# Attention cores: head 0 from SBUF, outputs kept in SBUF, one transfer per maximum, a banded core of its own, and an fp4 quantiser summed by TensorE

## The chip, the cores and the metric

The kernel runs on one core of a Trainium2 chip as one launch. TensorE (PE) multiplies matrices, VectorE (DVE), ScalarE (ACT) and GpSimd (POOL) work element by element, and SyncE's queue (SP) issues most transfers. The metric is the device time in microseconds, the median of several executions. SBUF is the on-chip memory of 128 partitions, PSUM the memory that matmuls write, DRAM lies off the core.

## The reference, cut to what matters

Tokens `x` (2048 of width 128) pass through eight residual layers, each `x = x + f(layernorm(x))`. The change touches the three attention layers with 16 heads of width 8 and the fp4 feed-forward layer.

```python
# L0 attention: each query sees itself and the 127 keys before it (banded)
scores = einsum('bhnqd,bhnkd->bhnqk', qb, kb) / sqrt(8); scores = where(allowed, scores, NEG)
out = einsum('bhnqk,bhnkd->bhnqd', softmax(scores), vb)        # allowed: 0 < distance <= 128
# L1 attention: the same over all keys, energy / sqrt(128).  L2 attention: causal, k <= q
# L0 feed-forward
def fp4_quant_dequant(x):            # blocks of 16 along the last dimension
    scale = maximum(max(abs(xb)) / 6.0, 1e-12)
    idx = searchsorted([0.25, 0.75, 1.25, 1.75, 2.5, 3.5, 5.0], abs(xb / scale))
    return [0.0, 0.5, 1.0, 1.5, 2.0, 3.0, 4.0, 6.0][idx] * sign(xb) * scale
h = silu(fp4_linear(x, w_gate)) * fp4_linear(x, w_up)           # hidden width 352
return fp4_linear(h, w_down)         # fp4_linear quantises both operands
```

## The kernel before

The program is a sequence of stages (`Stage`, one block of instructions for all engines each). A stage ends with a barrier of all engines, so nothing of one stage overlaps the next. The order of the work within a stage is written out by hand, engine by engine; semaphores join the engines, and each engine takes its own instructions strictly in order.

**An attention layer** is `layernorm_transpose`, `attention_front`, a core, `attention_normalise` and a projection. `attention_front` makes q, k and V for all heads. q and k are split into three bf16 parts each, so that nine bf16 products give an fp32 score, and the parts are stored to DRAM (`qparts`, `kparts`) by 12 transfers on SP (L1263). A core then treats head after head in two passes. Pass A computes all scores of the head with queries on the partitions, and DVE reduces each row to its maximum. The negated maxima are split in three bf16 parts, transposed by PE, copied to SBUF (`mT`) and laid by three transfers into rows 72 to 74 of `qh`, opposite three rows of ones in `kh`. Pass B computes the scores again, keys on the partitions, now with 75 rows, so that the maximum is already subtracted; ScalarE takes the exponential into `prob`. A third group of matmuls (L479, L791, L1117) multiplies `prob` with V and a column of ones into `psV`, four column chunks at partitions 0, 32, 64 and 96; ScalarE copies `psV` to `oh`, and SP stores output and denominators to DRAM in eight transfers a head. `attention_normalise` loads both back (L1380, L1381), inverts the denominators, spreads them with PE and multiplies.

The loads of `qh` and `kh` for a head broadcast the parts from DRAM on SP. Two or more heads are in flight: while PE does pass B of one head it takes units of pass A of the next in fixed slots (in the full-attention core 33 slots a head spread over 16 key blocks, the last one of which holds three), and the slot of the maxima transposition stands among them.

- The banded core (`attention_core`, stage l0a_core) treats a head as 31 blocks of 128 x 128: for each query block its own key block and the one before. In both passes each block gets a mask by a matmul of the identity with a 128 x 128 mask (L446, L467). Units are four blocks in A and eight in B. DVE reduces per query block (L578) and also splits the maxima (L590 to L596). POOL fills four `kh` with ones first (L410), 1.8 us each, and SP's first load waits for that.
- `wide_attention_core` (l1a_core) and `causal_attention_core` (l2a_core) have no masks in B; in the causal one POOL zeroes 16 diagonal blocks a head by `affine_select` (L1043). POOL splits the maxima in both (L1034 to L1037). DVE fills three `kh` with ones.

**fp4.** `Fp4` quantises a tile of 16-wide blocks: ScalarE takes magnitude and sign, DVE block maxima (L2067), scale (L2068), its inverse (L2069), the product with it (L2070), then counts thresholds in a chain of fused passes, `acc = (mag > mid) + acc` (L2072 to L2078), with one of the comparisons on POOL (L2053) while DVE does L2073, and ends with sign and scale (L2080, L2081). `l0_ffn` has stage l0w (weights 128 x 1120 and x, 128 x 2048) and stage l0h (hidden activations in four chunks of 128 x 1408: gate and up matmuls L2176, silu L2224, product L2247, quantisation, 12 transpositions L2185, ScalarE's copies L2214, 24 fp32 matmuls L2192, addition to X L2240).

## Time and profile before

Three executions took 3268.23, 3273.67 and 3277.10 us.

| what | us |
|---|---|
| median of three | 3273.67 |
| profiled execution, its own time | 3280.04 |
| its span in the trace | 3277.9 |
| ScalarE busy, POOL busy (whole span) | 1518.9, 549.0 |

Stages that the change touches, first to last instruction in the trace (us from the start of the span):

| stage | from | to |
|---|---|---|
| l0a_front (banded layer: projections, parts) | 31.55 | 61.68 |
| l0a_core | 62.49 | 317.02 |
| l0a_norm | 318.94 | 329.75 |
| l0w (fp4 weights and x) | 432.96 | 484.49 |
| l0h (fp4 hidden) | 485.26 | 611.19 |
| l1a_front (full attention) | 623.06 | 647.63 |
| l1a_core | 651.25 | 1420.22 |
| l1a_norm | 1422.16 | 1432.98 |
| l2a_front (causal) | 1746.61 | 1802.44 |
| l2a_core | 1805.67 | 2329.69 |
| l2a_norm | 2331.65 | 2343.42 |

Busy times count instructions that work, not the issuing of transfers. Matmuls are pipelined: one that is listed with 0.22 us starts 0.06 us after the one before it. A clock of 1.00 is TensorE's full 2.4 GHz, 0.5 is 1.2 GHz. What stands in brackets at the end of a row is how long the engine had been idle and what ended that.

### The profile page before, as it was taken

The page shows a single profiled execution, that of the slowest core. Times are in us where ns is not written, and L with a number is a line of the kernel's source. Part 1 is how long each engine was busy: PE and PEld are TensorE (multiplying, and loading weights), DVE is VectorE, ACT ScalarE, POOL GpSimd, SP SyncE. Part 2 cuts the span into 40 slices and gives each one's busy share as a digit, 9 for nine tenths or more (in the row PEclk, how much of TensorE's full clock was granted, in tenths as well). Part 3 has the DMA queues.
Part 4 walks back from the last instruction along what each step waited for, and adds up shares of the span by engine and source line. Part 5 has one row for each costly group of instructions (what it writes and reads, how often), then busy time and mean ns, then how long its engine had stood idle before and what let it go on. Part 6 is the DMA issues. An engine that isn't in the chain of part 4 may idle for free. (4 is left out here: it accounts for less than half of the span.)

```text
span 3277.9 us, 45624 instructions
## 1 busy us (share of the span) xinstructions
PE 2517.5 (77%) x16417; PEld 1220.7 (37%) x16417; DVE 1984.8 (61%) x3063; ACT 1518.9 (46%) x3040; POOL 549.0 (17%) x843
## 2 busy tenths in 40 slices
PE   2998523459999999957995799999677886766478
PEld 1776222312222222125674233333245545534423
DVE  2553477678888888531114677776285384458655
ACT  1232212217778777733432366666356356432211
POOL 3000011000000000000001111111174174104045
PEclk8998657659999999978997699999689998977689
DMA  2111000111111111002001000000110010000000
GB/s 69 47 50 40 1 9 0 44 56 39 38 37 39 43 43 43 3 17 52 1 1 38 29 23 26 26 26 11 46 34 5 1 30 2 1 6 2 1 20 13
DMA packets 57227, 82.88 MB, mean 25 GB/s; under 512 B 23114, under 2 KB 35564, under 8 KB 56620
## 3 DMA queue, kind: packets, MB, share of 16 engines
q1 hardware_dynamic: 57004, 79.97, 7.8%
q8 instruction: 132, 2.16, 0.3%
q14 instruction: 91, 0.75, 0.1%
HBM read 65.32 MB, written 14.02 MB: 24 GB/s over the span
## 5 line engine op out<-in xcount | busy, mean ns | idle before, releaser
L849 DVE TENSOR_REDUCE l1a_core_mpart<-l1a_core_psA 128x1 f32<-128x1024 f32 x512 | 601.5, 1220 | 96.8 <-PE l1a_core_psA L769 96.8
L831 ACT ACTIVATE l1a_core_prob<-l1a_core_psB 128x512 f32<-128x512 f32 x1024 | 552.1, 595 | 206.0 <-PE l1a_core_psB L780 204.4
L1159 ACT ACTIVATE l2a_core_prob<-l2a_core_psB 128x384 f32<-128x384 f32 (+3 forms) x656 | 316.0, 525 | 196.7 <-PE l2a_core_psB L1101 191.9
L1181 DVE TENSOR_REDUCE l2a_core_mpart<-l2a_core_psA 128x1 f32<-128x1024 f32 (+7 forms) x384 | 335.5, 909 | 118.0 <-PE l2a_core_psA L1088 68.0
L780 PE MATMUL l1a_core_psB<-l1a_core_qh,l1a_core_kh 75*128 75x512 bf16 x1024 | 312.0, 387 | 4.7 <-ACT l1a_core_prob L831 4.7
L791 PE MATMUL l1a_core_psV<-l1a_core_prob,l1a_core_vh 128*32 128x512 f32 x2048 | 274.4, 608 | 7.0 <-ACT l1a_core_oh L823 6.9
L769 PE MATMUL l1a_core_psA<-l1a_core_ka,l1a_core_qa 64*128 64x512 bf16 x1024 | 173.2, 403 | 67.9 <-DVE l1a_core_mpart L849 36.4
L1084 PE MATMUL l2a_core_psA<-l2a_core_kh,l2a_core_qh 72*128 72x512 bf16 (+3 forms) x640 | 181.3, 367 | 36.7 <-DMA l2a_core_kh<-kparts 31.3
L1101 PE MATMUL l2a_core_psB<-l2a_core_qh,l2a_core_kh 75*128 75x384 bf16 (+3 forms) x688 | 206.9, 349 | 2.8 <-DMA l2a_core_qh<-l2a_core_mT 2.6
L1117 PE MATMUL l2a_core_psV<-l2a_core_prob,l2a_core_vh 128*32 128x128 f32 (+3 forms) x1856 | 195.2, 444 | 15.0 <-ACT l2a_core_prob L1159 9.4
L1860 DVE SCALAR_TENSOR_TENSOR X<-l1e_psO,W,X 128x128 f32<-128x128 f32 x128 | 36.0, 344 | 220.6 <-PE l1e_psO L1817 220.6
L780 PEld LDWEIGHTS l1a_core_psB<-l1a_core_qh,l1a_core_kh 75*128 75x128 bf16 x1024 | 60.6, 97 | 292.6 <-ACT l1a_core_prob L831 271.6
L1849 ACT ACTIVATE l1e_h<-l1e_psH,l1e_b 128x512 f32<-128x512 f32 x128 | 87.9, 687 | 137.3 <-PE l1e_psH L1810 137.1
L1810 PE MATMUL l1e_psH<-XnT,l1e_w 128*128 128x512 f32 x256 | 118.6, 610 | 22.3 <-DMA l1e_b<-in_L_ffn_be 19.5
L1043 POOL TENSOR_SCALAR_AFFINE_SELECT l2a_core_prob<-l2a_core_prob 128x128 f32<-128x128 f32 x256 | 73.7, 292 | 359.3 <-ACT l2a_core_prob L1159 358.0
L578 DVE TENSOR_REDUCE l0a_core_mpart<-l0a_core_psA 128x1 f32<-128x128 f32 (+1 forms) x368 | 94.9, 329 | 57.0 <-PE l0a_core_psA L446 56.7
L557 ACT ACTIVATE l0a_core_prob<-l0a_core_psB 128x1024 f32<-128x1024 f32 x64 | 63.8, 998 | 138.1 <-PE l0a_core_psB L467 138.1
L769 PEld LDWEIGHTS l1a_core_psA<-l1a_core_ka,l1a_core_qa 64*128 64x128 bf16 x1024 | 45.9, 93 | 217.9 <-issue 112.6
L1817 PEld LDWEIGHTS l1e_psO<-l1e_w,l1e_h 128*128 128x128 f32 x1024 | 118.7, 192 | 13.4 <-issue 13.4
L1101 PEld LDWEIGHTS l2a_core_psB<-l2a_core_qh,l2a_core_kh 75*128 75x128 bf16 x688 | 62.2, 98 | 152.5 <-ACT l2a_core_prob L1159 90.3
L1817 PE MATMUL l1e_psO<-l1e_w,l1e_h 128*128 128x128 f32 x1024 | 118.8, 275 | 0.0
L2847 PE MATMUL l2f_qkv_psP<-l2f_w,XnT 128*128 128x512 f32 x192 | 96.2, 643 | 9.1 <-DVE V L2938 6.2
(632 smaller groups left out, 4444.4 us busy)
## 6 DMA issues: line engine op xcount, KB each, us to landing
l1a_core_qa<-qparts SPq DMA_DIRECT2D x64, 96.0 KB
l1a_core_ka<-kparts SPq DMA_DIRECT2D x32, 192.0 KB
l0a_core_kh<-kparts SPq DMA_DIRECT2D x48, 96.0 KB
l0a_core_qh<-qparts SPq DMA_DIRECT2D x48, 96.0 KB
l1a_core_qh<-qparts SPq DMA_DIRECT2D x48, 96.0 KB
l1a_core_kh<-kparts SPq DMA_DIRECT2D x16, 288.0 KB
l2a_core_qh<-qparts SPq DMA_DIRECT2D x48, 96.0 KB
l2a_core_kh<-kparts SPq DMA_DIRECT2D x16, 288.0 KB
```

The source lines that it names most:

```text
L769: ins = mm(ps[:, e * CH:(e + 1) * CH], qa[h % 2][rows, qb * P:(qb + 1) * P], ka[h % 2][rows, lo + e * CH:lo + (e + 1) * CH], start=True, s ...
L780: mm(psB[u % 3][:], kh[h % 3][0:QKM_ROWS, kb * P:(kb + 1) * P], qh[h % 3][0:QKM_ROWS, c * CH:(c + 1) * CH], start=True, stop=True).then_in ...
L791: ins = mm(psV[32 * c:32 * c + 32, :], vh[h % 2][:, kb, :], prob[(u + c) % (2 * PER_KB)][:], start=kb == 0, stop=kb == NT - 1, skip_group_ ...
L831: nc.scalar.activation(prob[u % (2 * PER_KB)][:], psB[u % 3][:], ACT.Exp, scale=scale).then_inc(b_exped, 1)
L849: nc.vector.tensor_reduce(mpart[:, n // 2, n % 2:n % 2 + 1], psA[i % 2][:], AX.X, ALU.max).then_inc(a_freed, 1)
L1084: ins = mm(ps[:, at * P:(at + nb) * P], qh[h % 3][0:QK_ROWS, place * P:(place + 1) * P], kh[h % 3][0:QK_ROWS, kb * P:(kb + nb) * P], start ...
L1101: ins = mm(out.rearrange("p (c n) -> p c n", c=groups), kh[h % 3][0:QKM_ROWS, kb * P:(kb + 1) * P], q4[:, c:c + groups, first * P:CH], sta ...
L1117: ins = mm(psV[32 * (c + i):32 * (c + i) + 32, first * P:CH], vh[h % 2][:, kb, :], prob[(NB * h + u) % RING][:, lo * P:(lo + 4 - first) * ...
L1159: nc.scalar.activation(prob[n % RING][:, 0:cols], psB[n % 3][:, 0:cols], ACT.Exp, scale=scale).then_inc(b_exped, 1)
L1181: ins = nc.vector.tensor_reduce(mpart[:, place, part:part + 1], psA[i % 2][:, lo * P:hi * P], AX.X, ALU.max)
L1810: nc.tensor.matmul(psH[j][:], w1[:, e, j * P:(j + 1) * P], xs, start=True, stop=True).then_inc(hid_done, 1)
L1817: ins = nc.tensor.matmul(psO[e % 2][:, t * P:(t + 1) * P], h[e % 2][:, j, t * P:(t + 1) * P], w2[:, e, j, :], start=j == 0, stop=j == J - ...
```

## The change

1. A new stage object `FirstHead` spans front and core. It owns the buffers `qh`, `kh` (for full attention also `qa`, `ka`) of head 0. The front fills them straight from its own q and k parts: `kh` is set to 1.0 by DVE, q rows by transfers on SP, k rows by transfers on ScalarE's queue (9 each, 16 each with `halves`). The front waits for them at its end. The cores skip the load of head 0; the rows of ones of the other `kh` buffers are copied by one transfer each.
2. A head's outputs go by four transfers to `g.CT` and one to `g.den`, both in SBUF. `attention_normalise` loads nothing.
3. The maxima go to `qh` by one transfer instead of three.
4. The banded layer has its own core, `window_attention_core`. In A a unit is four query blocks; two matmuls of the identity with a 512-column mask come first and four score matmuls of 256 columns are added; DVE reduces a unit in one instruction. In B there is no mask; a unit is two key blocks with two query blocks each, eight units a head, and POOL zeroes what lies outside the band by two `affine_select` per unit. POOL also splits the maxima. The values run in four waves, three B units late.
5. Full and causal attention: head 0's maxima come after one unit of head 1 instead of four; in full attention the slots are two per key block with the third beside the maxima slot, and the copy of the output comes two exponentials earlier.
6. fp4: seven comparisons make 0/1 tiles in bf16 (five on DVE, two on ScalarE as Sign then Relu); seven bf16 matmuls with 0.5, 1 or 2 times the identity sum them in PSUM; DVE multiplies by the sign from PSUM, then by the scale. POOL has no part. l0w treats x in two halves; l0h is reordered.

```diff
+class FirstHead(Stage):
+    def __init__(self, nc, name, halves=False):
+        self.qh, self.kh = [self.sb(n, [P, S], BF16) for n in ("qh", "kh")]
+        self.fills = 32 if halves else 18
+    def fill_q(self, eng, i, part):
+        for lo in (0, 64) if self.halves else (0,):
+            for j in range(2 if self.halves and i == 2 else 3):
+                at = lo + HD * (3 * i + j)
+                eng.dma_start((self.qa if self.halves else self.qh)[at:at + HD, :], part[0:HD, :]).then_inc(self.filled, 16)
...
+def store_head(sp, g, h, oh, stored):
+    for c in range(NC):
+        sp.dma_start(g.CT[h * HD:(h + 1) * HD, c * CH:(c + 1) * CH], oh[32 * c:32 * c + HD, :]).then_inc(stored, 16)
+    sp.dma_start(g.den[h * HD:(h + 1) * HD, :], oh[HD::32, :].rearrange("c (s j) -> c s j", j=SEG)).then_inc(stored, 16)
+def load_maxima(sp, qh, mT, loaded):
+    sp.dma_start(qh[QK_ROWS:QK_ROWS + 3, :].rearrange("i (t j) -> i t j", j=P), mT[:]).then_inc(loaded, 16)
...
 # window_attention_core, PE, a unit of A
+                for e in range(2):
+                    mm(ps[:, e * CH:(e + 1) * CH], g.identb[:], (g.window_q if n + e else g.window_q0)[:], start=True,
+                       stop=False, skip_group_check=True)
+                for i in range(4):
+                    qb = 4 * n + i
+                    oldest = max(qb - 1, 0)
+                    ins = mm(ps[:, (2 * i + 2) * P - (qb + 1 - oldest) * P:(2 * i + 2) * P], qh[b][0:QK_ROWS, qb * P:(qb + 1) * P],
+                             kh[b][0:QK_ROWS, oldest * P:(qb + 1) * P], start=False, stop=True, skip_group_check=True)
 # POOL, a unit of B
+            def zero_outside(h, u):
+                pool.wait_ge(b_exped, NB * h + u + 1)
+                p = prob[u][:].rearrange("p (k e n) -> p k e n", e=2, n=P)
+                behind = columns(u) // P - 2
+                own, after = p[:, :, 0, :], p[:, 0:behind, 1, :]
+                nc.gpsimd.affine_select(out=own, in_=own, compare_op=ALU.is_ge, fill=0.0, base=-1,
+                                        pattern=[[0, 2], [1, P]], channel_multiplier=-1).then_inc(zeroed, 1)
+                nc.gpsimd.affine_select(out=after, in_=after, compare_op=ALU.is_ge, fill=0.0, base=-1,
+                                        pattern=[[0, behind], [-P, P]], channel_multiplier=P + 1).then_inc(zeroed, 1)
+            for h in range(H):
+                if h + 1 < H:
+                    split_maxima(h + 1)
+                for u in range(NB):
+                    zero_outside(h, u)
+                    if u == 4 and 2 <= h + 1 < H:
+                        lay_v(h + 1)
 # PE, a wave of values
+                pe.wait_ge(zeroed, 2 * NB * h + 4 * j + 4)
...
 # wide_attention_core
-                    while done < min(end, first + per_head * (kb + 1) // NT):
+                    while done < min(end, begin + 2 * (kb + 1) + (turned_by[min(h + 1, H - 1)] - 1 < begin + 2 * (kb + 1))):
-                    if n == 5 and h:
+                    if n == 3 and h:
                         copy_o(h - 1)
...
 # class Fp4
+    MIDS = (2.5, 3.5, 5.0, 1.25, 1.75, 0.25, 0.75)
+    STEPS = (1.0, 1.0, 2.0, 0.5, 0.5, 0.5, 0.5)
+    def above_on_dve(self, j):
+        self.nc.vector.tensor_scalar(self.above[j][:], self.mag[:].rearrange("p n q -> p (n q)"), self.MIDS[j], None,
+                                     ALU.is_gt).then_inc(self.dve_above, 1)
+    def add_up(self, pe, out, lo, n, turn=0):
+        for j, t in enumerate(self.above):
+            ins = self.nc.tensor.matmul(out, self.consts.step[self.STEPS[j]][:], t[:, lo:lo + n], start=j == 0, stop=j == 6)
 # l0h, PE: the order of the chunks
+            for c in range(NC):
+                if c + 1 < NC:
+                    for t in range(4 * c + 4, 4 * c + 8):
+                        inputs(t)
+                add_up(c)
+                if c:
+                    down(c - 1)
 # l0h, DVE: chunk c
+                if c >= 2:
+                    add_out(c - 2)
+                q.block_maxima(dve, turn)
+                hidden(ahead)
+                q.scales(dve, turn)
...
+                for t in range(4):
+                    dve.wait_ge(summed, 4 * c + t + 1)
+                    q.sign(hid[c % 3][:, t, :], psQ[t % 2][:, 0:FF], t * FF, FF).then_inc(signed, 1)
+                q.multiply(blocks(c)).then_inc(multiplied, 1)
```

## Rows read from the trace of the kernel before

**Rows 1.** Page, busy microseconds by engine, share of the span, and instructions.

```profile
PE 2517.5 (77%) x16417; PEld 1220.7 (37%) x16417; DVE 1984.8 (61%) x3063; ACT 1518.9 (46%) x3040; POOL 549.0 (17%) x843
```

**Rows 2.** Busy time by stretch: window, its length, PE, PEld, DVE, ACT, POOL, clock, DMA share, GB/s.

```profile
62.50:318.90 256.40, 218.89 (x2288) 165.69 (x2288) 116.12 (x480) 74.66 (x81) 12.98 (x26) 0.93 0.15 44
137.00:153.00 16.00, 15.44 (x166) 11.35 (x163) 8.34 (x36) 5.15 (x6) 0.59 (x2) 1.00 0.20 57
...
433.00:484.50 51.50, 5.79 (x25) 4.65 (x25) 45.94 (x26) 9.77 (x13) 10.98 (x3) 0.53 0.04 11
485.20:611.20 126.00, 52.96 (x208) 38.56 (x208) 93.65 (x72) 25.26 (x37) 17.85 (x4) 0.65 0.00 0
...
803.80:847.70 43.90, 42.33 (x257) 9.17 (x257) 38.18 (x37) 34.98 (x65) 1.12 (x5) 1.00 0.12 40
...
2500.00:2540.00 40.00, 30.19 (x540) 25.21 (x538) 24.31 (x42) 28.75 (x119) 20.00 (x22) 1.00 0.01 2
```

**Rows 3.** Groups of instructions in the banded core; count, then busy us, mean ns, idle before.

```profile
L578 DVE TENSOR_REDUCE l0a_core_mpart<-l0a_core_psA 128x1 f32<-128x128 f32 x240 | 61.9, 284 | 57.0 <-PE l0a_core_psA L446 56.7
...
L578 DVE TENSOR_REDUCE l0a_core_mpart<-l0a_core_psA 128x1 f32<-128x256 f32 x128 | 53.1, 415 | 0.0
```

**Rows 4.** Timeline of PE in one head of the banded core: start, duration, instruction.

```profile
152.34 0.28 PE L460 MATMUL l0a_core_psB<-l0a_core_qh,l0a_core_kh 75*128 75x256 bf16 x1
152.46 0.22 PE L467 MATMUL l0a_core_psB<-cur_k,identb 128*128 128x128 bf16 x1
...
153.34 2.81 PE L479 MATMUL l0a_core_psV<-l0a_core_prob,l0a_core_vh 128*32 128x256 f32 x20
...
166.01 0.28 PE L460 MATMUL l0a_core_psB<-l0a_core_qh,l0a_core_kh 75*128 75x256 bf16 x1
```

**Rows 5.** Groups of instructions on POOL over the whole span.

```profile
L1043 POOL TENSOR_SCALAR_AFFINE_SELECT l2a_core_prob<-l2a_core_prob 128x128 f32<-128x128 f32 x256 | 73.7, 292 | 359.3 <-ACT l2a_core_prob L1159 358.0
...
L1365 POOL TENSOR_TENSOR V<-V,l0a_front_bvr 128x2048 f32<-128x2048 f32 x1 | 11.3, 11307 | 38.5 <-ACTq L1245 38.5
...
L1360 POOL TENSOR_SCALAR_AFFINE_SELECT l2a_front_gather<-l2a_front_gather 128x1024 f32<-128x1024 f32 x4 | 8.0, 2004 | 0.3
...
L1037 POOL TENSOR_TENSOR l2a_core_mb<-l2a_core_mrest,l2a_core_mb 128x16 bf16<-128x16 f32 x16 | 3.5, 218 | 1.3
```

**Rows 6.** Timeline of PE, the first matmul of each attention core, with the idle time before.

```profile
79.97 0.27 PE L439 MATMUL l0a_core_psA<-l0a_core_kh,l0a_core_qh 72*128 72x128 bf16 x1 [30.39 <-DMA l0a_core_qh<-qparts]
...
670.27 0.61 PE L769 MATMUL l1a_core_psA<-l1a_core_ka,l1a_core_qa 64*128 64x512 bf16 x2 [30.94 <-DMA l1a_core_ka<-kparts]
...
1818.54 0.59 PE L1084 MATMUL l2a_core_psA<-l2a_core_kh,l2a_core_qh 72*128 72x512 bf16 x1 [31.28 <-DMA l2a_core_kh<-kparts]
```

**Rows 7.** Timeline of DVE, its first instruction after the full-attention core.

```profile
1424.87 0.29 DVE L1396 TENSOR_SCALAR l1a_norm_den<-l1a_norm_den 128x256 f32<-128x256 f32 x1 [57.52 <-DMA l1a_norm_den<-den_dram]
```

**Rows 8.** Timeline of ACT in key block 15 of one head, full-attention core.

```profile
1021.57 1.08 ACT L831 ACTIVATE l1a_core_prob<-l1a_core_psB 128x512 f32<-128x512 f32 x2 [0.45 <-PE l1a_core_psB L780]
...
1024.14 1.09 ACT L831 ACTIVATE l1a_core_prob<-l1a_core_psB 128x512 f32<-128x512 f32 x2 [1.49 <-PE l1a_core_psB L780]
...
1025.67 2.16 ACT L831 ACTIVATE l1a_core_prob<-l1a_core_psB 128x512 f32<-128x512 f32 x4 [0.45 <-PE l1a_core_psB L780]
```

**Rows 9.** Groups of instructions on DVE in the fp4 hidden stage.

```profile
L2078 DVE SCALAR_TENSOR_TENSOR l0h_h0acc<-l0h_h0mag,l0h_h0acc 128x1408 f32<-128x1408 f32 x6 | 9.8, 1625 | 0.2
...
L2073 DVE SCALAR_TENSOR_TENSOR l0h_h1acc<-l0h_h1mag,l0h_h1acc 128x1408 f32<-128x1408 f32 x2 | 8.8, 4399 | 0.1
...
L2072 DVE TENSOR_SCALAR l0h_h0acc<-l0h_h0mag 128x1408 f32<-128x1408 f32 x2 | 1.8, 894 | 0.1
```

**Rows 10.** Timeline of DVE, start and end of the fp4 hidden stage.

```profile
493.83 0.52 DVE L2247 TENSOR_TENSOR l0h_hid<-l0h_sg,l0h_psU 128x352 f32<-128x352 f32 x1 [0.66 <-ACT l0h_sg L2224]
...
599.73 1.63 DVE L2081 TENSOR_TENSOR l0h_hid<-l0h_h1acc,l0h_h1scale 128x1408 f32<-128x1408 f32 x1
...
610.50 0.69 DVE L2240 TENSOR_TENSOR X<-X,l0h_psO 128x512 f32<-128x512 f32 x1 [8.43 <-PE l0h_psO L2192]
```

948 lines of the change are left out of this document (474 added, 474 removed).

## The prediction

> **What bounds the kernel now.** I read the page's busy shares first: TensorE (PE) 77% [rows 1]. The kernel is a row of stages with a barrier after each, so an average decides nothing. The busy time by stage does [rows 2]; in it the reader is to compare each engine's busy time with the length of the stretch. In the banded core PE works 15.44 of 16.00 us at clock 1.00 while GpSimd (POOL) works 0.59: PE is the bound there. In the fp4 hidden stage VectorE (DVE) works 93.65 of 126 us and in the fp4 weights stage 45.94 of 51.5: DVE is the bound. In the full-attention core PE works 42.33 of one head's 43.90 us and DVE 38.18: both are near full. Then the timeline at the edges of stages: each core begins with PE waiting 30 us for a load [rows 6], each normalising stage with DVE waiting for one [rows 7].
>
> Sums are made against the profiled execution (3280.04 us, span 3277.9).
>
> **Banded core (318.94 - 62.5 now).** Sixteen heads at about 13.7 us: 152.34 to 166.01 [rows 4]. A bf16 matmul of 256 columns costs PE 0.12 us from start to start (152.34 to 152.46), and a burst of 20 fp32 value matmuls 2.81 [rows 4]. The new core leaves out every mask matmul in B and puts two 512-column ones per unit in A. A per head: 4 x (1024 mask + 1024 score columns) at 0.115 per 256 = 3.7 us with the transposition. B: 31 blocks, 1.8. Values: 12 calls of 256 columns and 7 of 128 where there were 24 and 14; 38 cost two bursts of about 2.7, so half is 2.4 with the waits between waves. PE: 7.9 us.
> DVE does 4 reduces of 1024 elements; 128 and 256 elements cost 0.284 and 0.415 [rows 3], so 1.2 each, with the maxima's copy and scaling 5.3. ScalarE has 4.7 us a head now (74.66 / 16 [rows 2]); eight smaller instructions make it 5.4.
> POOL gets the band: per head 15 selects of 256 elements and one of 128. None of 256 is in the trace. 128 costs 0.292 and 1024 costs 2.004 [rows 5], 1.91 ns an element, so 0.54: 15 x 0.54 + 0.29 = 8.4. Split of the maxima, four instructions at 0.20 to 0.22 [rows 5]: 0.8. Copy of V 0.3. Twelve waits at about 0.04: 0.5. Sum 10.0 us: **POOL is the new bound**, PE idles 2 us a head. Bounds: a select of 0.45 would give 8.6, near PE's own floor; one of 0.66 (more than two of 128) 12. I take 0.54, since both neighbours lie on one line.
> Start: no 7 us of memsets and no wait to 79.97 [rows 6]. A(0) starts at about 62.6, at half clock as PE has idled: four units at 1.7, one of head 1 (its load lands by about 71), split 1.2, transposition, copy and one transfer about 4; three more units fill that. B begins at 79, where it began at 92.8. Then 16 x 10.0, the last wave, copy, five stores at 0.3 and their landing 5: the next stage starts at 244, not 318.9: **-75** (bounds -40 and -95).
>
> **Head 0 fed from SBUF.** Fronts gain 9 (16) DMA issues on SP and as many on ScalarE's queue, each 0.3 to 0.7 us, mostly beside the parts still being made; the front waits for their landing. In the first front POOL's 11.3 us on V [rows 5] end last and hide them. I take +0.5, +2, +1 (sum bounds +1 and +12). In exchange PE starts at once in the full-attention core, not at 670.27 (stage start 651.25): -18.8; in the causal one not at 1818.54 (1805.67): -12.7 [rows 6]. The loads of head 1 have 35 us and more to land. **+3.5 - 31.5 = -28.**
>
> **Outputs in SBUF.** The three normalising stages lose two loads: DVE starts 2.7 us after the load is issued [rows 7], 2.0 and 2.8 in the others: **-7.2**. Five instead of eight stores at the end of a core: 3 x 0.3, twice (the third is in the banded sum): **-1.8**. One transfer for three per maximum saves 1 us of SP's queue, hidden behind the slots that follow.
>
> **Full attention, steady.** In key block 15 PE has three score slots: its four exponentials take 4.10 us (1021.57 to 1025.67), with ScalarE idle 1.49 in between [rows 8]; 43.90 less 4.10 leaves 2.65 for each of the other fifteen. The third slot moves beside the cheap maxima slot, where DVE has only a 0.22 us copy: -1.3 x 14 heads; copying the output two exponentials earlier -0.1: **-20** (bounds -26, and -10 if key block 14 then spills).
>
> **fp4 hidden.** A chunk is now ten passes of DVE over 1408 elements: 4.4 us for the one that meets POOL, 1.63 for each other fused one [rows 9], and the last ends at 601.36 [rows 10]. New DVE work: maxima 1.6, scales 0.9, divide 1.6, five compares at 0.89 [rows 9], four products with hidden at 0.52, four signs of the same shape 2.1, multiply 1.6: 14.5. But the signs wait for PE: seven matmuls of 352 columns per tile, about 1.1 us at full and 2.1 at half clock (0.65 in this stage [rows 2]), two banks: 4.4 to 8.4 instead of 2.1. A cycle is 18.2 to 22.3; I take 19.6. Two costs come on top. DVE's first instruction of chunk c adds the output of c-2, and PE runs that down-projection only after the sums of c-1: its 12 transpositions, copies and 24 fp32 matmuls took 9.1 us at the end of the stage (601.4 to 610.5 [rows 10]); 8 assumed, as the clock is between its levels, 2 of it covered: DVE stalls 5.8 + 0.7 for chunks 2 and 3, with everything behind it on its queue. And two down-projections run one after the other at the end. The first chunk's last product is at 493.83 [rows 10]; magnitudes 1.4, then a cycle: 516. The others end at 535.6, 561.7 and 586 (no products in the last); two down-projections, 2 covered, and the addition: 600.5. Now 611.2: **-11** (0 to -22).
>
> **fp4 weights.** A fused pass over both operands is 3.6 us (2048 and 1120 elements, at the rate of rows 9). Six such passes (21.9) and the slow one over both (9.9, at the rate of 4.40) go; four more compares at 2.0 and one sign pass come: 45.9 - 21.9 - 9.9 + 8 + 3.7 = 26. Sums of the weights that nothing covers, at half clock (0.53 [rows 2]), +5.5; start and last transpositions +5.2: 36.7 for 51.5: **-14.8** (-8 to -19).
>
> **Causal core, steady:** same instructions: 0 (-3 to +3).
>
> Sum: -75 - 28 - 7.2 - 1.8 - 20 - 11 - 14.8 = **-158**, so 3122 for the profiled execution; that lies 6.4 above the median shown: **3116**.
>
> **A rule against it.** DVE's pass beside POOL's compare took 4.40 us, the same pass alone 1.63 [rows 9]. The Trainium skill ("SBUF — State Buffer", SBUF: two separate sides) says the two engines share a port pair under an exclusive lock, taken also by DVE instructions with two SBUF inputs. Row and rule agree in kind; in the new banded core DVE reads its scores from PSUM, so by the rule POOL's longer stay costs it nothing, and the sum stands. If the slowing of rows 9 came all the same, the two would take turns: 5.3 + 8.4 is 13.7 us a head, 60 us of the 75 would be gone and the time 3176; the causal core's DVE and selects, beside each other, show no such pair in the rows I read, and I hold that to be inside the range.
>
> **Rivals.**
> *A, PE's clock.* PE will idle before POOL in every head. If the clock then stands at its lower level (1.2 for 2.4 GHz), PE's 7.9 becomes about 15.5 and is the bound: +5.5 x 16 = +88, and up to +100 with the ends: 3210. For it: the fp4 stage, with PE 42% busy, shows 0.65. Against it: at 2500 to 2540 PE is 75% busy and the clock 1.00 [rows 2], and PE would be near 79% busy here. The skill ("TensorE: Matmul & The Clock Gate", Part 1) tells of kernels whose PE idles shortly between groups and whose clock then swings; row 2500 speaks against it here. 7%.
> *B, the other side.* The selects have a pattern of two dimensions, one of them with a negative step, and nothing in the trace has its price at 256 elements. At 0.82 us each the head costs 14.3, as now; at 1.2 it costs 20.0 and the 158 us are gone; at 1.3 the time is 3290. POOL serves all heads in series, so nothing hides it. Against: a 1024-element select with groups costs 1.96 ns an element [rows 5]. 2%.
> *C, the small terms fail.* fp4 hidden gains nothing (clock low in its sums, output stall whole), fp4 weights -8, the full-attention period stays: -158 + 11 + 7 + 20 = -120: 3154. 18%.
> *D, more.* Select 0.45 (-22), hidden stage at full clock (-8), full attention -26 for -20: 3080. 12%.
> *E, the change doesn't do what it says:* a front waits for its fills as long as the core waited (+5.5 each over my terms, and head 1's loads stall): 3135. 5%.
> Forecast 56%.
>
> **Numbers.** 3116; forecast alone 3095 to 3140. Eight in ten: 3070 to 3180, which takes in C, D, E and part of the way to A. Less than 0.3% (10 us) can't be told from no change: faster 0.96, same 0.01, slower 0.03.
>
> **What would show it.** Banded core: POOL over 90% busy between selects, PE idle on POOL, about 10.0 us a head; a select row of 0.54. First PE instruction within 1 us of each core's start. Key block 15 with pairs of exponentials 2.15 us apart. In the hidden stage DVE idle about 6 us before the addition to X at chunks 2 and 3. Wrong if the select costs over 0.8 us, if the clock in the banded core is under 0.9, or if a front grows by over 6 us.

## The result and the profile after

The changed kernel takes 3165.2 us (median of 4 runs, 3157.65 to 3181.59) against 3272.43 (4 runs, 3268.23 to 3277.1) for the kernel before: ratio 0.968, 95% interval 0.964 to 0.972. The sign and the rough size were right. The time lies within the range, but 49 us above the forecast, so two of my terms are far off.

The profiled execution took 3157.65 us (span 3155.2); it answers to the one of before with 3280.04 (span 3277.9). First the page of the kernel after: busy microseconds, share and instructions of each engine, and the granted clock in 40 slices.

```profile
PE 2478.2 (79%) x15554; PEld 1139.8 (36%) x15554; DVE 1888.7 (60%) x2695; ACT 1560.4 (49%) x3134; POOL 620.7 (20%) x1148
PEclk8886687599999999979986999997889989978689
```

PE lost 39 us of work and DVE 96 [rows 1]; POOL gained 72. The gain of 107 is not in one of these numbers. The time of each stage, from its first instruction to that of the next, shows where it is (worked out from both traces, us):

| stage | before | after | difference | forecast |
|---|---|---|---|---|
| three attention fronts | 118.2 | 155.5 | **+37.3** | +3.5 |
| banded core | 256.5 | 204.3 | **-52.2** | -75 |
| full-attention core | 770.9 | 728.0 | -42.9 | -39.7 |
| causal core | 526.0 | 515.4 | -10.6 | -13.6 |
| three normalising stages | 35.7 | 28.1 | -7.7 | -7.2 |
| fp4 weights | 52.3 | 36.2 | -16.1 | -14.8 |
| fp4 hidden | 127.1 | 110.6 | -16.5 | -11 |
| sum | | | **-108.7** | -158 |

The forecast column deals the step "head 0 from SBUF" and the stores out to the stages in which they act. The remaining 14 us between the two spans are in stages of unchanged code, which other runs of that code show at other lengths (the layer with local attention, from `local_qkv` to `local_ffn`, took 512 us here, 518 to 527 in the twelve runs below and 519 before); the median difference, 107, fits the sum without them. Fronts and banded core miss by 34 and 23 us; all the others together are 7.5 us better than forecast.

The busy time by stretch of the kernel after, with the columns of [rows 2]: the banded core whole; 16 us of it that answer to the second row of [rows 2]; fp4 weights; fp4 hidden; one head of the full-attention core.

```profile
70.00:274.40 204.40, 162.93 (x1264) 80.45 (x1264) 83.09 (x96) 80.26 (x145) 113.19 (x341) 0.78 0.15 51
150.00:166.00 16.00, 13.20 (x111) 6.95 (x114) 7.06 (x9) 7.51 (x14) 10.41 (x31) 0.83 0.21 73
383.00:418.60 35.60, 17.96 (x74) 8.12 (x74) 27.70 (x41) 21.87 (x28) 0.45 (x1) 0.72 0.06 16
418.60:529.00 110.40, 66.33 (x320) 42.27 (x320) 57.26 (x76) 47.83 (x53) 0.00 (x0) 0.83 0.00 0
1018.90:1061.10 42.20, 42.17 (x258) 9.42 (x257) 38.17 (x36) 35.06 (x66) 1.11 (x5) 1.00 0.12 42
```

In the banded core POOL is busy 113 of 204 us, not over 90%: the new bound of my forecast isn't there. PE is busy 163 us at a mean clock of 0.78 instead of 0.93. Two groups of instructions say what the band costs, POOL's two selects of the banded core (count, then busy us, mean ns, idle before):

```profile
L424 POOL TENSOR_SCALAR_AFFINE_SELECT l0a_core_prob<-l0a_core_prob 128x256 f32<-128x256 f32 x128 | 52.0, 406 | 60.0 <-ACT l0a_core_prob L539 59.4
L426 POOL TENSOR_SCALAR_AFFINE_SELECT l0a_core_prob<-l0a_core_prob 128x256 f32<-128x256 f32 x112 | 45.5, 406 | 0.0
```

A select of 256 elements takes 0.406 us, not 0.54, below even the lower bound that I gave it. POOL waits for ScalarE, 60 us in all.

What holds PE instead stands in its waits from 100 to 230 us (total, times, longest), and in its timeline. The second fence has the start of the core, where [rows 6] had a wait of 30 us, two further waits, and the first of the periodic ones.

```profile
PE l0a_core_psB L485 <- issue: 13.1, 6, 2.4
PE l0a_core_psA L459 <- POOL l0a_core_mb L416: 3.8, 6, 0.6
```

```profile
70.39 1.04 PE L466 MATMUL l0a_core_psA<-window_q,identb 128*128 128x512 bf16 x2 [21.27 <-POOL l0a_core_mb L429]
...
80.64 1.01 PE L466 MATMUL l0a_core_psA<-window_q,identb 128*128 128x512 bf16 x2 [4.29 <-DMA l0a_core_kh<-kparts]
...
88.81 0.43 PE L485 MATMUL l0a_core_psB<-l0a_first_qh,l0a_first_kh 75*128 75x256 bf16 x2
95.04 1.01 PE L466 MATMUL l0a_core_psA<-window_q,identb 128*128 128x512 bf16 x2 [5.80 <-DMA l0a_core_kh<-kparts]
...
113.75 0.33 PE L485 MATMUL l0a_core_psB<-l0a_core_qh,l0a_core_kh 75*128 75x256 bf16 x2
116.26 0.59 PE L485 MATMUL l0a_core_psB<-l0a_core_qh,l0a_core_kh 75*128 75x256 bf16 x2 [2.19 <-issue]
```

PE starts 0.27 us after the core does, as forecast. But twice in the start it waits for the load of a next head, and then in every second head it stands for 2.0 to 2.4 us at the start of the second pass ("B"). "issue" names no releaser. The code leaves only one: the first score matmul of B waits for the transfer of the row maxima into the q tile (the semaphore that it waits for gets its last increment 0.09 us before it). SP's timeline around it shows the order of the issues:

```profile
105.17 2.12 SPq L364 DMA_DIRECT2D l0a_first_qh<-qparts  x3
107.33 0.68 SPq L366 DMA_DIRECT2D l0a_first_kh<-kparts  x1
108.26 0.72 SPq L303 DMA_DIRECT2D l0a_core_qh<-l0a_core_mT  x1
```

The 12 KB of maxima are issued at 108.26, right behind four transfers (576 KB) of the load of a later head, and their last part lands at 116.17 in the trace's records, 7.9 us later; 0.09 us later PE goes on. In the kernel before, the order was the other way round, maxima first and the load behind them:

```profile
156.66 1.83 SPq L372 DMA_DIRECT2D l0a_core_qh<-l0a_core_mT  x3
158.53 0.55 SPq L365 DMA_DIRECT2D l0a_core_kh<-kparts  x1
```

There the transfers of the maxima landed 1.6 to 3.2 us after their issue, 1.7 in the median. So the changed kernel turned this order round, which neither the description of the change nor the prediction says.

What such a stall does to PE is seen in three stretches: before it, from it on, and after (same columns; the last but two is the clock).

```profile
104.90:116.20 11.30, 8.36 (x82) 4.36 (x80) 6.59 (x8) 5.43 (x10) 8.72 (x28) 1.00 0.17 62
116.20:126.00 9.80, 9.74 (x71) 4.70 (x71) 3.28 (x4) 3.90 (x7) 4.27 (x13) 0.65 0.18 66
126.00:138.50 12.50, 9.54 (x96) 5.09 (x89) 7.11 (x9) 6.03 (x12) 9.72 (x30) 1.00 0.19 59
```

At full clock until the stall; then PE has next to no idle time, and its clock stands at the lower level (0.50) for 6.8 us, 0.65 in the mean of the stretch; then full again. All six stalls have such a fall within 1.7 us of their end; the falls last 3.4 to 10.2 us. That is rival A's event in a form that I hadn't seen: not PE idling before POOL, but PE idling for a transfer. The Trainium skill ("TensorE: Matmul & The Clock Gate", Part 1) describes kernels whose clock swings between its two levels because PE idles between groups of matmuls. This trace agrees in kind, with 2.2 us of idling in front of the lower level.

The other side of the balance is the front of full attention, SP's and ScalarE's queues. "x6" are six copies of 32 KB each from the part tile into head 0's tiles:

```profile
559.47 6.41 SPq L90 DMA_DIRECT2D l1a_first_qa<-l1a_front_partq  x6
565.92 1.23 SPq L1219 DMA_DIRECT2D kparts<-l1a_front_partk  x1
567.20 1.28 SPq L1219 DMA_DIRECT2D qparts<-l1a_front_partq  x1
568.52 8.08 SPq L90 DMA_DIRECT2D l1a_first_qa<-l1a_front_partq  x6
...
579.43 4.32 SPq L90 DMA_DIRECT2D l1a_first_qa<-l1a_front_partq  x4
...
587.53 0.76 SPq L635 DMA_DIRECT2D l1a_first_qh<-qparts  x1
```

```profile
559.54 19.88 ACTq L97 DMA_DIRECT2D l1a_first_ka<-l1a_front_partk  x16
```

Thirty-two copies, 1.05 MB, are issued from 559.5 to 583.1, and the core (587.5) begins behind them. The busy time from 560 to 580, and the GB/s that the DMA moved from 559 to 588 us, in 40 slices:

```profile
560.00:580.00 20.00, 0.00 (x0) 0.00 (x0) 5.19 (x6) 0.00 (x0) 0.00 (x0) 0.50 0.57 99
```

```profile
GB/s 88 251 381 79 45 45 51 51 51 45 62 51 122 187 251 107 138 105 51 51 45 45 51 57 51 51 57 124 195 283 127 73 88 71 51 59 212 136 0 0
```

PE, ScalarE and POOL do nothing, DVE works 5.19 us: little is left beside which the copies could hide. The peaks are the stores of the parts to DRAM; where copies go alone, the row stands at 45 to 57 GB/s.

The ends of the cores and the fp4 hidden stage, as far as the forecast named them: the last copy and stores of the banded core; the copy of the output, twice, in the full-attention core (43.90 us apart before); DVE's additions to X in the hidden stage.

```profile
267.53 0.60 ACT L531 ACTIVATE l0a_core_oh<-l0a_core_psV 128x512 f32<-128x512 f32 x1 [2.01 <-PE l0a_core_psV L501]
268.15 2.99 SPq L298 DMA_DIRECT2D CT<-l0a_core_oh  x4
271.19 0.57 SPq L299 DMA_DIRECT2D den<-l0a_core_oh  x1
274.42 0.29 DVE L1351 TENSOR_SCALAR den<-den 128x256 f32<-128x256 f32 x1 [23.99 <-PEq L62]
```

```profile
1018.87 0.60 ACT L782 ACTIVATE l1a_core_oh<-l1a_core_psV 128x512 f32<-128x512 f32 x1 [0.16 <-PE l1a_core_psV L750]
...
1061.05 0.60 ACT L782 ACTIVATE l1a_core_oh<-l1a_core_psV 128x512 f32<-128x512 f32 x1 [0.16 <-PE l1a_core_psV L750]
```

```profile
469.70 0.69 DVE L2308 TENSOR_TENSOR X<-X,l0h_psO 128x512 f32<-128x512 f32 x1 [4.55 <-PE l0h_psO L2242]
...
495.85 0.69 DVE L2308 TENSOR_TENSOR X<-X,l0h_psO 128x512 f32<-128x512 f32 x1 [6.25 <-PE l0h_psO L2242]
...
527.28 0.69 DVE L2308 TENSOR_TENSOR X<-X,l0h_psO 128x512 f32<-128x512 f32 x1 [6.11 <-PE l0h_psO L2242]
```

### The profile page after: what moved, and what is told of

Same layout as the page of the kernel before. It is cut to its first block and busy times, and to the rows that moved or that the text cites. A ratio compares the mean times of both kernels' runs of the same rounds, so it can differ in the third digit from the quotient of the medians.

```text
span 3155.2 us, 43935 instructions
## 1 busy us (share of the span) xinstructions
PE 2478.2 (79%) x15554; PEld 1139.8 (36%) x15554; DVE 1888.7 (60%) x2695; ACT 1560.4 (49%) x3134; POOL 620.7 (20%) x1148
## 5 line engine op out<-in xcount | busy, mean ns | idle before, releaser
L739 PE MATMUL l1a_core_psB<-l1a_core_qh,l1a_core_kh 75*128 75x512 bf16 x640 | 193.7, 384 | 0.8 <-ACT l1a_core_prob L790 0.8
L556 DVE TENSOR_REDUCE l0a_core_mrow<-l0a_core_psA 128x4 f32<-128x1024 f32 x64 | 78.2, 1224 | 108.4 <-PE l0a_core_psA L471 108.4
L1767 PE MATMUL l1e_psH<-XnT,l1e_w 128*128 128x512 f32 x256 | 118.7, 610 | 22.3 <-DMA l1e_b<-in_L_ffn_be 19.5
L539 ACT ACTIVATE l0a_core_prob<-l0a_core_psB 128x512 f32<-128x512 f32 (+1 forms) x128 | 71.3, 583 | 115.7 <-PE l0a_core_psB L485 115.7
L1059 PE MATMUL l2a_core_psB<-l2a_core_qh,l2a_core_kh 75*128 75x384 bf16 (+3 forms) x430 | 127.1, 341 | 0.0
L726 PE MATMUL l1a_core_psA<-l1a_first_ka,l1a_first_qa 64*128 64x512 bf16 x512 | 89.0, 412 | 46.6 <-POOL l1a_core_mb L691 30.3
L739 PE MATMUL l1a_core_psB<-l1a_first_qh,l1a_first_kh 75*128 75x512 bf16 x384 | 117.9, 390 | 4.3 <-ACT l1a_core_prob L790 4.3
L1040 PE MATMUL l2a_core_psA<-l2a_core_kh,l2a_core_qh 72*128 72x512 bf16 (+3 forms) x400 | 110.1, 357 | 0.8 <-DVE l2a_core_mpart L1137 0.8
L739 PEld LDWEIGHTS l1a_core_psB<-l1a_core_qh,l1a_core_kh 75*128 75x128 bf16 x640 | 37.5, 97 | 173.5 <-ACT l1a_core_prob L790 161.5
```

What stands on the lines that cost most here:

```text
L739: mm(psB[u % 3][:], kh[h % 3][0:QKM_ROWS, kb * P:(kb + 1) * P], qh[h % 3][0:QKM_ROWS, c * CH:(c + 1) * CH], start=True, stop=True).then_in ...
L1040: ins = mm(ps[:, at * P:(at + nb) * P], qh[h % 3][0:QK_ROWS, place * P:(place + 1) * P], kh[h % 3][0:QK_ROWS, kb * P:(kb + nb) * P], start ...
L1059: ins = mm(out.rearrange("p (c n) -> p c n", c=groups), kh[h % 3][0:QKM_ROWS, kb * P:(kb + 1) * P], q4[:, c:c + groups, low * P:CH], start ...
L1767: nc.tensor.matmul(psH[j][:], w1[:, e, j * P:(j + 1) * P], xs, start=True, stop=True).then_inc(hid_done, 1)
```

## The experiments

All are edits of the changed kernel; ratios are against the kernel before, on the same chip. The runs stand on three chips, on which the kernel before takes 3273 to 3287 us, so small differences are read from ratios and stages, not from microseconds of the whole. Stage times are from each one's trace. Two questions: what holds the banded core at 204 us, and where the 37 us of the fronts come from and whether the feed earns them.

### Banded core: the maxima transfer on another queue

```diff
-            load_m(0)                      # SyncE's queue
             load_qk(2)
             for h in range(H):
                 if h + 3 < H: load_qk(h + 3)
-                if h + 1 < H: load_m(h + 1)
...
+            load_m(0)                      # ScalarE's queue
...
                     if u == LATE and h: copy_o(h - 1)
+                    if u == LATE and h + 1 < H: load_m(h + 1)
```

> The changed kernel, with the banded core's maxima transfer issued on ScalarE's queue (behind the fourth exponential) instead of SyncE's; load of head 2 no longer waits behind the maxima of head 0. Theory A (the transfer of a head's maxima lands 8 us after its issue because it stands behind the 4 broadcast loads of SyncE's queue; TensorE stalls 2.0 to 2.4 us at every second head and its clock then falls to the lower level for most of that head): the six stalls go, the mean granted clock of the banded core rises from 0.78 to over 0.9, a head takes about 9 us in all of them, and the stage is 25 to 35 us shorter than 204. Rival B (GpSimd's selects bound the core, as the prediction had it): the stage stays within 5 us. Rival C (the stall is something else, instruction loading for instance): the stalls stay at 2 us.

Measured: 3172.38 us (3150.06 to 3175.04), ratio 0.966 (0.962 to 0.970), as the changed kernel itself. The core takes 206.0 us, and all six stalls are still there: theory A, as I had put it, missed, and the 25 to 35 us didn't come. Its waits of PE, 100 to 230 us:

```profile
PE l0a_core_psB L478 <- issue: 15.3, 6, 3.0
```

The maxima of this kernel are issued at 104.81, 1.1 us behind the end of SP's issues of the load (100.89 to 103.72), on a queue with nothing before them, and PE still goes on only at 112.85, 8.0 us after. So the wait is not a place in SP's queue; it is in something that both queues share. The trace's packet records show what it looks like. On SP's queue (the changed kernel) the 48 packets of 256 bytes begin 6.7 us after the issue, all within 0.8 us, behind the load's. On ScalarE's queue they begin 4.2 us after it and are strewn over 3.2 us, between packets of the load. The Trainium skill says ("DMA: Bandwidth & Descriptors", Issuing engines are not separate DMA queues) that transfers started by several engines end up on the same 16 DMA engines and interleave there. This run agrees: they interleave, and land no sooner. It isn't that all 16 engines are full: between issue and landing their mean busy share is 0.22 and 0.24. Which shared part makes the packets wait, no run here shows.

### Banded core: without the selects

```diff
-                nc.gpsimd.affine_select(out=own, ...).then_inc(zeroed, 1)
-                nc.gpsimd.affine_select(out=after, ...).then_inc(zeroed, 1)
...
-                pe.wait_ge(zeroed, 2 * NB * h + 4 * j + 4)
```

The probabilities outside the band are not set to zero here.

> The changed kernel without the 16 selects per head on GpSimd in the banded core, so what lies outside the band stays in the sums. Theory A (a select of 256 elements takes 0.41 us, GpSimd is busy 8 of 11 us a head, and TensorE with its stalls is the bound): the core is at most 12 us shorter, the stalls at every second head stay. Rival B (GpSimd is the bound, as the prediction had it): the core is over 25 us shorter.

Measured (one execution): 3171.9 us, core 205.7. POOL's busy time in 130 us falls from 81.60 to 13.11 us and the core doesn't move; PE's six waits at the start of B stay too (12.5 us). The stretch from 100 to 230 us of this kernel:

```profile
100.00:230.00 130.00, 111.58 (x910) 55.96 (x909) 60.30 (x69) 56.74 (x103) 13.11 (x59) 0.84 0.18 60
```

That takes POOL out as the bound of the changed kernel; whether the selects cost something once the stalls are gone, this run can't say. It also tests the rule of the port lock that I weighed ahead: DVE's reduces of 1024 elements take 1224 ns here, and 1224 ns with the selects beside them. The Trainium skill ("SBUF — State Buffer", SBUF: two separate sides) gives the lock to DVE instructions that have two SBUF inputs or run in a mode with two ports. By that a reduce from PSUM doesn't take it, and these two numbers agree.

### Banded core: a fifth buffer, and the loads behind the maxima

```diff
-    NA, LEAD, GAP, NB, LATE, BUFS = 4, 4, 1, 8, 3, 4
+    NA, LEAD, GAP, NB, LATE, BUFS = 4, 4, 1, 8, 3, 5
...
+            load_qk(2)
             load_m(0)
-            load_qk(2)
+            load_qk(3)
             for h in range(H):
-                if h + 3 < H: load_qk(h + 3)
                 if h + 1 < H: load_m(h + 1)
+                if h + 4 < H: load_qk(h + 4)
```

Each load is issued one head further ahead and just behind the maxima, not just before them. The run changes both at once.

> The changed kernel; in the banded core five buffers for q and k instead of four, the loads one head further ahead, and in each head the maxima transfer issued before the loads. Theory D (the maxima land 6 to 8 us after their issue because the 16 DMA engines are still writing the 576 KB of the load issued before it, on whichever queue they were issued; in a head at full clock, 8.9 us, that is too late for the next head, TensorE stalls 2 us and falls to its lower clock for a head of 11 to 13 us): the maxima land within 3 us, the stalls at every second head go, nearly all heads take about 9 us and the core is 20 to 30 us shorter than 204; the granted clock of 100 to 240 us goes over 0.9. Rival C (the stalls have another cause, or the load itself needs more than a head's time): stalls of about 2 us stay, at the same or at other instructions, and the core keeps its length within 6 us.

Measured: 3126.04 us (3123.0 to 3126.9), ratio 0.951 (0.950 to 0.953). The core takes 177.05 us, 27.3 less. SP's timeline, PE's waits from 100 to 230 us, and the busy time from 100 to 230 and from 150 to 166 us:

```profile
122.35 0.77 SPq L303 DMA_DIRECT2D l0a_core_qh<-l0a_core_mT  x1
123.17 2.17 SPq L364 DMA_DIRECT2D l0a_core_qh<-qparts  x3
125.38 0.69 SPq L366 DMA_DIRECT2D l0a_core_kh<-kparts  x1
```

```profile
PE l0a_core_psA L460 <- POOL l0a_core_mb L417: 9.5, 13, 1.8
```

```profile
100.00:230.00 130.00, 117.35 (x1102) 61.07 (x1101) 69.30 (x81) 70.28 (x129) 99.40 (x298) 0.95 0.19 62
150.00:166.00 16.00, 14.89 (x139) 7.84 (x137) 9.34 (x11) 8.77 (x17) 12.24 (x38) 1.00 0.24 78
```

From 100 to 230 us the DMA moves 62 GB/s in both kernels; the order and the distance of the loads are what changed. The maxima land 3.9 us after the issue (3 expected), and "issue" is gone from the waits. Twelve heads in a row take 8.95 us between two copies of the output, where the changed kernel had heads of 9.0 to 13.2. The 5.80 us wait at 95.04 is gone too, since the load of head 2 is no longer behind the maxima of head 0. From 150 to 166 us PE works 14.89 of 16 us, at clock 1.00, and POOL 12.24. One head, and the wait that it has left:

```profile
150.50:159.44 8.94, 8.12 (x82) 4.35 (x80) 5.19 (x6) 4.94 (x10) 6.98 (x22) 1.00 0.22 73
157.58 0.22 PE L460 MATMUL l0a_core_psA<-identb,l0a_core_mb 128*128 128x128 bf16 x1 [0.65 <-POOL l0a_core_mb L417]
```

PE works 8.12 us of a head and waits 0.65 for POOL's split of the maxima and 0.17 for a select. The clock stays at 1.00 from 104.16 to 220.21 us with such waits in every head; a wait of 1.79 us ends at 220.20, and behind it the clock is at 0.50 to the end of the core.

The two traces differ by 30.0 us: 27.3 in this stage and 12.4 in the causal core (503.0 against 515.4), less 11.8 in the layer with local attention; those two have the same code in both kernels, and some 2 us lie elsewhere. In the causal core the clock was at 0.50 for 37.6 us over the last heads of the changed kernel, and for 3.4 us here. That part is luck. The medians differ by 39 us and the ratios by 0.017, or 54 us (the kernel before took 3272 us beside the one and 3287 beside the other); only the 27 are shown to be the edit's.

### Fronts: no feed at all

```diff
-                        if half and which == 0: feed.fill_q(sp, i, parts[0][i])
-            sp.wait_ge(feed.filled, 16 * feed.fills)
...
-                feed.fill_k(act, j, parts[1][j])
...                                        # in each core
+            load_qk(0)
```

> The changed kernel without the fills of head 0: the three fronts issue none, and the cores load head 0 from DRAM as the others. Theory A (each transfer that writes SBUF takes about 0.68 us of a descriptor generator that both issuing queues share, so 18, 32 and 18 fills lengthen the fronts by 9, 19 and 9 us and eat what the cores gain): fronts as in the kernel before (31, 28, 59 us from start to the core's start), cores longer by 9 to 12 (banded), 15 to 19 (full), 9 to 13 us (causal); in sum within 8 us of the changed kernel. Rival B (fronts grew for another reason, the memset or the wait for ScalarE): the fronts keep 10 us or more of their 37.

Measured: 3154.18 us (3142.96 to 3158.35), ratio 0.962 (0.959 to 0.965), no slower than with the feed. Front and core together, banded, full and causal: 238.1, 775.8 and 571.9 us; with the feed 243.9, 775.5 and 583.7. Of the last, 12.3 us are the low clock of the last heads, which this run didn't have; with them taken as equal it is 571.4. The banded core is 2.7 us longer than with the feed, not the 9 to 12 expected. The fronts are back at 31.1, 29.2 and 59.2, and PE's first matmul (full attention) at

```profile
587.91 1.04 PE L726 MATMUL l1a_core_psA<-l1a_first_ka,l1a_first_qa 64*128 64x512 bf16 x4 [30.65 <-DMA l1a_first_ka<-kparts]
```

that is 19.2 us after the core starts, and at the same absolute time as with the feed (587.80). In the full-attention layer the copies into SBUF take as long as the load through DRAM that they replace: the wait has moved from the core into the front. In the banded core the feed loses 6 us.

### Fronts: all copies on one queue

```diff
+                        elif half:
...
+                            feed.fill_k(sp, i, parts[1][i])
...
-                feed.fill_k(act, j, parts[1][j])           # ScalarE's queue
```

> The changed kernel with all fills of head 0 issued on SyncE's queue, none on ScalarE's. Theory A (one generator shared by both queues, 0.68 us per fill): an issue now takes 0.7 instead of 1.3 us, and the fronts are as long as before to within 3 us. Rival B (1.3 us is what such a transfer costs its own queue): the full-attention front grows by another 15 to 20 us.

Measured (one execution): 3161.44 us, fronts 38.2, 46.6 and 69.0, within 1.5 us of the changed kernel's. On one queue a copy is issued every 0.66 to 0.69 us (six of them in the line below); on two, one every 1.1 to 1.35 on each (above: 6.41 us for six, 19.88 for sixteen):

```profile
558.55 4.14 SPq L90 DMA_DIRECT2D l1a_first_qa<-l1a_front_partq  x6
```

Two queues issue no more per microsecond than one, for copies into SBUF. So either the issues have one shared rate, or both show the back-pressure of the copies' own speed. The next runs tell these apart.

### Fronts: half the bytes, and twice the copies

The first keeps the number of copies and halves each one; head 0's other columns hold ones:

```diff
-                eng.dma_start(...[at:at + HD, :], part[0:HD, :])
+                eng.dma_start(...[at:at + HD, S // 2:S], part[0:HD, S // 2:S])
```

> The changed kernel with the same 18, 32 and 18 fills of head 0, but each copies only the second half of the columns (the first half holds ones, so head 0 is computed from other values). Theory A (a fill costs its issue, 0.68 us, whatever its size): the three fronts stay within 3 us of 39.6, 47.5 and 68.4. Theory V (what counts is the bytes written to SBUF, 1.05 MB in the full-attention front, which took 19 us both as 32 copies and as the loads of the core, 53 GB/s): the fronts take about 35, 38 and 64 us.

The second copies everything in twice as many halves, the first ones as soon as the first half of the columns is made:

```diff
-                        if half and which == 0: feed.fill_q(sp, i, parts[0][i])
+                        if which == 0: feed.fill_q(sp, i, parts[0][i], cols)
...
-            self.fills = 32 if halves else 18
+            self.fills = 64 if halves else 36
```

> The changed kernel with each fill of head 0 in two, one for each half of the columns, issued as soon as that half of the parts is made (36, 64 and 36 fills). Theory A: the fronts grow by another 12 (banded, causal) and 20 us (full attention). Theory V: the bytes are the same and half of them start 6 to 7 us earlier: the fronts take 34 to 37, 41 to 44 and 63 to 66 us.

Half the bytes (one execution, as the second): 3143.11 us, fronts 33.8, 35.8 and 64.5. The full-attention front is 11.7 us shorter; its 16 copies on ScalarE's queue:

```profile
552.69 11.96 ACTq L102 DMA_DIRECT2D l1a_first_ka<-l1a_front_partk  x16
```

against 19.88 above. Twice the copies: 3163.44 us, fronts 37.2, 47.2 and 68.5, neither the gain nor the loss that was expected; the 64 copies begin 9 us earlier (550.62) and the last is issued 2 us earlier (581.07). From the first issue to the last it is 23.7 us for 32 whole copies, 14.1 for 32 halves, 30.5 for 64 halves. The first two give 0.14 us a copy and 18 us a megabyte (55 GB/s), an estimate from two runs; that makes 28 for the third. Most of the feed's cost is its bytes, at about 50 GB/s, and a smaller part is their number. So the 1.2 us an issue on two queues is the copies' own speed pressing back: with half the bytes it is 0.75 (11.96 / 16).

### Fronts: head 0 through DRAM, but inside the front

```diff
+            act.wait_ge(q_stored[i], 32)       # the parts' stores have landed
+            act.dma_start(self.qa[lo:lo + n * HD, :], g.qparts[i:i + 1, 0:HD, :].broadcast_to([n, HD, S]))
...                                        # 10 loads for 32 copies, 4 for 18
```

> The changed kernel with head 0 brought to SBUF by the broadcast loads from DRAM (4, 10 and 4 transfers on ScalarE's queue), but inside the front, each as soon as its parts are stored, in place of the 18, 32 and 18 copies from SBUF. Theory A (what a fill costs is its 0.68 us of issue, whatever its size, so fewer and larger transfers are cheaper though they go by DRAM): the fronts take 36 to 38, 36 to 39 and 64 to 66 us (39.6, 47.5 and 68.4 with the copies; 31.1, 29.2 and 59.2 with none), the cores keep their early start, and the kernel is 12 to 20 us faster than the changed one. Rival (the way by DRAM is as long as the copies): fronts within 3 us of the copies'.

Measured: 3171.04 us (3151.2 to 3184.69), ratio 0.967 (0.963 to 0.970); fronts 39.1, 44.5 and 68.5. I expected them clearly shorter than with the copies; only the middle one is, by 3 us. The last of its ten loads is issued at 569.51 and the core starts at 581.6:

```profile
569.51 0.44 ACTq L101 DMA_DIRECT2D l1a_first_ka<-kparts  x1
```

With issues of 0.44 to 0.73 us and ten transfers in place of 32, the end stays where it was. Either way the megabyte takes some 20 us.

### Full attention: the old slots

```diff
-                    while done < min(end, begin + 2 * (kb + 1) + (turned_by[...] - 1 < begin + 2 * (kb + 1))):
+                    while done < min(end, begin + per_head * (kb + 1) // NT):
```

> The changed kernel with the distribution of the score slots of the full-attention core as before (33 slots over 16 key blocks by proportion, three in the last); the output copy stays two exponentials earlier. Theory F (the third slot in key block 15 costs about 1.4 us a head, the later copy 0.3): a head takes 43.5 to 43.7 us instead of 42.19, the core 19 to 21 us more than 728. Rival (the earlier copy is what gained the 1.71 us a head): the head stays under 42.7.

Measured (one execution): 3185.17 us; a head takes 43.39 us, 0.1 under the 43.5 to 43.7 expected, against 42.19, and the core 747.25, +19.2. The head of before had 43.90; I put the 0.5 us between down to the earlier copy of the output, but no run has that edit alone.

### fp4 hidden: the addition to X behind the compares

```diff
-                if c >= 2: add_out(c - 2)
                 q.block_maxima(dve, turn)
...
                 q.above_on_dve(4)
+                if c >= 2: add_out(c - 2)
```

> The changed kernel; in the fp4 hidden stage the addition of chunk c-2's output stands behind the five comparisons of chunk c on VectorE, not ahead of the chunk. Theory E (VectorE stands 4.55 and 6.25 us at chunks 2 and 3 before that addition, waiting for the down-projection, with the whole chunk behind it): the stage falls from 110.5 to 99 to 103 us. Rival (TensorE's down-projection is then late for the sums of chunk c, and the wait moves there): 107 to 111.

Measured (one execution): the stage takes 103.61 us for 110.55, -6.9 of the 10.8 that DVE idled; 0.6 above the expected 99 to 103. The time of the whole, 3167.76, can't show it. DVE in this kernel: the additions to X come without a wait, and part of it turns up at the products with the sums instead.

```profile
486.45 0.68 DVE L2308 TENSOR_TENSOR X<-X,l0h_psO 128x512 f32<-128x512 f32 x1
489.53 0.53 DVE L2049 TENSOR_TENSOR l0h_hid<-l0h_psQ,l0h_h0sgn 128x352 f32<-128x352 f32 x1 [2.40 <-PE l0h_psQ L2045]
```

### Together

Fifth buffer, late addition to X, and either no feed (first) or the feed in halves (second).

```diff
+ the edits of "a fifth buffer" and of "the addition to X behind the compares"
+ first: those of "no feed at all"; second: those of "twice the copies"
```

> The changed kernel with five buffers and the maxima ahead of the loads in the banded core, the addition to X behind the comparisons in the fp4 hidden stage, and no fills of head 0. By the stages of the runs before: banded front and core 31 + 180, fp4 hidden 103.5, full attention 29 + 747, causal 59 + 513: about 3110 us, 45 to 50 us faster than the changed kernel (ratio to the kernel before 0.945 to 0.950).

> The same as best_a, but head 0 is filled from SBUF by halves. By theory V the fronts gain 5 us each over whole fills: 3108 to 3115 us, within 8 us of best_a. By theory A: over 3150 us.

Measured: 3127.59 us (3111.34 to 3138.76), ratio 0.955 (0.950 to 0.960), and 3136.5 us (3120.89 to 3141.13), ratio 0.957 (0.952 to 0.961). Both missed the 3108 to 3115 that I expected, and neither, on another chip than the fifth buffer, beats the fifth buffer alone (0.951, 0.950 to 0.953). The stages that were edited came out as in the single runs (banded front and core 212.7 and 214.9, fp4 hidden 103.7 in both); the losses are in the full-attention core of the first (755.9 against 746.6 with the same code, one head of 47.09 us) and in the causal cores (519.3 and 515.2 against 503.0). Such swings of 9 to 17 us in the long cores, from one run to the next and with PE's clock, are as large as the terms that I tried to add up here.

## Why the prediction was right, and where it wasn't

**Banded core, POOL as the bound: wrong, in two ways that partly cancel.** The step from 0.292 us for 128 elements and 2.004 for 1024 to 0.54 for 256 failed: 0.406. That "both neighbours lie on one line" was no support, since any two points do. POOL needs 7.1 us a head (113.2 / 16), not 10.0, and leaving the selects out changes nothing while the stalls are there. PE's own work was sized about right, 8.1 for 7.9. But a head takes 8.95 at full clock: I had POOL's split of the maxima in POOL's sum only, and PE waits for its end, 0.65 us a head. With these two alone the core would have taken 177 us (the fifth buffer shows it) and the gain would have been 79, close to my 75 for the wrong reason. What cost 27 of it was not in the forecast: the transfer of the maxima waits behind a load of 576 KB. It costs 13.1 us of stalls in 130 us, a mean clock of 0.85 for 0.95 in the same stretch (0.50 for 6.8 us behind the stall shown), and 5.8 us at the start. I had counted the load of head 1 as landed by 71; PE waited for it until 80.64. I took "transposition, copy and one transfer about 4" for the landing and looked at nothing that lies in front of it, although the new kernel changed just that: before, the maxima were issued ahead of the load, landed in 1.7 us and had a head of 13.7 us to land in.

**Rival A, the clock.** I gave it 7% in a form (PE at low clock throughout, 3210) that didn't come. My argument against it, that a stretch with PE 75% busy stood at clock 1.00 [rows 2], was about the mean; as far as these traces show, what matters is how the idle time is cut up. With five buffers twelve of PE's 13 waits for POOL's maxima are 0.65 us or less and the clock is 1.00 over all of them; in the changed kernel a wait of 2.19 us was followed by 0.50, and with five buffers so was the thirteenth, of 1.79. Of the signs of being wrong that I had named two came: the clock in the banded core under 0.9 (0.78), and fronts that grow by over 6 us.

**Head 0 from SBUF: the mechanism half right, the price wrong; the step worth most of the miss.** The cores start as forecast (PE 0.27 us after the start in each; -18.5 and -12.7 to the first exponential, for -18.8 and -12.7). The step that failed is that the fronts' issues lie "mostly beside the parts still being made", and the +0.5, +2 and +1 taken for them: they gained 8.7, 19.3 and 9.3. In the first front POOL's work on V, which I had taken to end last and hide them, ends at 61.2, 8.9 us before the core. Rival E said it in words ("a front waits for its fills as long as the core waited") and had 5%, with +5.5 each where 8 to 17 over my terms came; I gave E the right event with a size that no row had. The size could have been read: the load that the copies replace kept PE waiting 19 us into the core [rows 6]; the same bytes into the same partitions should have been priced by it until something showed otherwise. By that the term would have been about 0 instead of -28, and the sum -130.

**Full attention:** -24 for -20: the head takes 42.19 us, which is 16 times 2.64, the 2.65 that I had read for a key block with two slots; block 15 no longer stands out. The run with the old slots gives 19 for the slots and leaves 0.5 us a head for all else in the steady core, the earlier copy among it, where I had 0.1.

**Outputs in SBUF:** -7.7 for -7.2: right. **Stores:** wrong in sign, small. I took 0.3 us for each of five; the issues take 0.57 to 0.65 each, where those to DRAM took 0.26. Together they last 3.6 us (268.15 to 271.76) where the eight of before lasted 2.4 (314.66 to 317.02), so a core loses 1.2 where I booked a gain of 0.9.

**fp4 weights:** -16.1 for -14.8, right. **fp4 hidden:** -16.5 for -11. The cycle is 19.7 us (19.6 forecast) and the two additions to X wait 4.55 and 6.25 us (5.8 each). Only the ends were sized too long: the first chunk ends 26.8 us into the stage, not 30.7, and the two down-projections at the end take 12.1, not 14.5. The clock was 0.83 in place of 0.65, with PE busy 60% of the stage for 42%; what that gave isn't separated. The bounds of the cycle, 18.2 to 22.3, don't follow from the terms beside them (16.8 to 20.8); they fit with the 1.4 of the magnitudes added.

**Causal core, steady:** -10.6 is -12.7 at the start, 1.2 for the stores and about 1 us worse than zero in between, inside the 3 that I allowed. Both kernels ran their last heads at the lower clock, 30.7 us before and 37.6 after. In rival B the time at 1.3 us a select should read 3298, not 3290; nothing rests on it.

**What stays open.** Why copies into these tiles run at about 50 GB/s, when stores of the parts in the same front reach 250 to 380. All of them read the same eight partitions and each writes eight; other partitions weren't tried. In the packet records a packet of 4096 bytes takes 0.63 us in the median where copies go alone (572 to 577 us, 49 GB/s, mean DMA share 0.47); in the loads that open the core of the run without the feed (569 to 588 us, 73 GB/s, share 0.20) it takes 0.16. So the two ways are not slow alike, and that both need some 20 us may be chance. Which of the two edits of the fifth-buffer run, order or distance, frees the maxima, and which part of the DMA they wait in. Why the long cores of unchanged code vary by 9 to 17 us between runs. Whether the two combined versions are better or worse than the fifth buffer alone: their intervals meet at 0.950 to 0.953.
